# A graph network on one core: without the instructions that carry a second wait in the hot loops, and with the second tables' empty rows written in layer 1's first pass

## What is computed

```python
x = x + L0(h)   # gaussian mixture: msg = sum_k gauss_k(edge) * (h @ g)[src], mean over dst, + h @ root + bias
x = x + L1(h)   # two SAGE convolutions: mean of h[src] by dst, dense layers, relu, again
x = x + L2(h)   # spline convolutions: a small network moves each edge's coordinates,
                # then z[col*K + idx] weighted by an 8-corner basis, summed by row
x = x + L3(h)   # two SAGE convolutions with sums in place of means
```

## Time and profile before

| what | value |
|---|---|
| median of three timed runs | 15050.08 us (15047.9 to 15058.99) |
| the profiled execution's own time | 15074.62 us |
| its span, first to last instruction | 15072.8 us |
| mean granted TensorE clock | 0.558 of full speed |
| instructions in the profile | 155974 |
| busy: PE, DVE, ACT, POOL | 7096.2, 5575.7, 1755.8, 8971.3 us |

### The profile page before, as it was taken

How to read it: one execution, slowest core, us unless ns; L and a number is a source line. 1 busy time by engine, 2 the same in 40 slices (tenths; PEclk the granted TensorE clock), 3 DMA queues, 4 the chain that set the end, 5 groups by cost and what they waited for, 6 DMA issues and landing times. The chain is left out here.

```text
span 15072.8 us, 155974 instructions
## 1 busy us (share of the span) xinstructions
PE 7096.2 (47%) x32816; PEld 6021.4 (40%) x32819; DVE 5575.7 (37%) x11340; ACT 1755.8 (12%) x5296; POOL 8971.3 (60%) x9011
## 2 busy tenths in 40 slices
PE   5200455556665555455557775444444453334333
PEld 1100344446663333344446664433333343333332
DVE  8200344444445666333335554333233341111111
ACT  0000333322221111000010001111111110000000
POOL 0677566636665555555526665666666526664666
PEclk9555666655557777555555555555555555555555
DMA  7991111123331111211121112000111121112112
GB/s 271 139 106 13 53 67 67 64 70 91 89 86 34 42 41 40 26 30 31 30 13 12 12 12 15 12 12 12 21 23 23 24 34 12 12 12 12 13 13 14
DMA packets 790129, 641.91 MB, mean 43 GB/s; under 512 B 363646, under 2 KB 680304, under 8 KB 789814
## 3 DMA queue, kind: packets, MB, share of 16 engines
q1 hardware_dynamic: 466548, 303.70, 11.4%
q0 software_dynamic: 295168, 243.14, 9.1%
q10 hardware_dynamic: 28288, 93.72, 1.6%
HBM read 264.86 MB, written 386.20 MB: 43 GB/s over the span
## 5 line engine op out<-in xcount | busy, mean ns | idle before, releaser
L802 PE MATMUL ps<-got,oh 128*128 128x33 f32 x7040 | 1670.1, 400 | 2383.0 <-DVE oh L625 675.8
L802 PEld LDWEIGHTS ps<-got,oh 128*128 128x128 f32 x7040 | 1573.8, 327 | 2547.0 <-issue 2531.9
L765 POOL DMA_INDIRECT got<-q_table,idx x1760 | 1809.7, 1028 | 1186.1 <-DVE idx L807 657.2
L2144 POOL DMA_INDIRECT msg<-msg,idx x1792 | 1759.0, 982 | 1126.1 <-issue 524.4
L765 POOL DMA_INDIRECT got<-h_table,idx x1760 | 1719.1, 977 | 1116.8 <-issue 569.9
L1703 POOL DMA_INDIRECT cell<-rec,idx x880 | 921.6, 1047 | 609.4 <-ACT rec L1685 352.1
L348 POOL DMA_INDIRECT rec_r<-sc_rec,sc_idx x832 | 840.8, 1011 | 721.3 <-ACT sc_rec L339 423.2
L1367 POOL DMA_INDIRECT rec_d<-rec,idx x880 | 908.6, 1032 | 563.6 <-ACT rec L1307 310.5
L1969 POOL DMA_INDIRECT cell<-rec,idx x880 | 912.9, 1037 | 498.7 <-issue 270.8
L625 DVE TENSOR_TENSOR oh<-iota_f,rd 128x512 f32<-128x512 f32 x1105 | 759.7, 692 | 1025.1 <-DMA b<-in_L_gnn_b 498.2
L807 DVE CAST idx<-rd 128x4 int32 (+1 forms) x892 | 158.1, 178 | 2441.6 <-DMA msg<-msg,idx 634.8
(11 more groups left out here) (329 smaller groups left out, 13359.1 us busy)
## 6 DMA issues: line engine op xcount, KB each, us to landing
got<-rec_d SPq DMA_DIRECT2D x220, 416.0 KB
rec_d<-padd ACTq DMA_DIRECT2D x4, 11648.0 KB
rec_d<-padd ACTq DMA_DIRECT2D x4, 11232.0 KB
cin<-cell SPq DMA_DIRECT2D x224, 136.0 KB
msg<-msg,idx POOLq DMA_INDIRECT x1792
msg<-zpad SPq DMA_DIRECT2D x8, 3575.0 KB
got<-msg SPq DMA_DIRECT2D x220, 130.0 KB
cell<-rec,idx POOLq DMA_INDIRECT x1760
```

Of the source, the lines that this page charges most:

```text
L765: nc.gpsimd.indirect_dma_start(out=s["got"][:, n, g, :], out_offset=None, in_=table, in_offset=bass.IndirectOffsetOnAxis(ap=s["idx"][:, n, ...
L802: mm = nc.tensor.matmul(psum_rows[:, ds(at[g], W)], s["oh"][:, n, g, :], s["got"][:, n, g, 0:W], start=False, stop=False)
L2144: nc.gpsimd.indirect_dma_start(out=msgs, out_offset=bass.IndirectOffsetOnAxis(ap=idx[:, n, g:g + 1], axis=0), in_=msg[:, n, g, :], in_offs ...
```

## The change

Two things. First, every `sem_inc(tick, 1)` of PE, ACT and DVE in the loops named above goes; the waits stay. POOL's ticks stay, and those in `layer_norm` and the dense stages. Second, the scatter's phase now blanks only `cell1` and `msg1`; `cell2` and `msg2` are blanked by ACT with the same 16 DMAs, each waited for, at the start of its part of layer 1's first pass. The small source tiles `pad2` and `zpad` live through the whole kernel for that.

```diff
+        def blank_tables(eng, sem, tables):
+
+            parts, filled = 8, 0
+            for table, pad, tiles in tables:
+                groups = tiles // 2
+                view = table.rearrange("(p t u) w -> p t (u w)", p=P, u=2)
+                for q in range(parts):
+                    t0, t1 = groups * q // parts, groups * (q + 1) // parts
+                    eng.dma_start(view[:, t0:t1, :], bcast(pad.unsqueeze(1), [P, t1 - t0, pad.shape[1]])).then_inc(sem, 16)
+                    filled += 16
+                    eng.wait_ge(sem, filled)
...
-                    parts, filled = 8, 0
-                    for table, pad, tiles in ((cell1, ...), (msg1, ...), (cell2, ...), (msg2, ...)):
...
+                    blank_tables(sp, s_filled, ((cell1, pad1[:, :, :].rearrange("p u w -> p (u w)"), TC),
+                                                (msg1, zpad[:, 0:2 * (F1 + 1)], TILES_N)))
...
             def act(eng):
+                if blank is not None:
+                    blank_tables(eng, s_blank, blank)
                 if t_nm is None:
                     return
                 with eng.Fori(0, NI) as i:
...
                         eng.wait_ge(picked, k + R - 1)
-                        nc.scalar.sem_inc(tick, 1)
...
                 pe.wait_ge(s["gathered"][n], 16 * G * (i + 1))
                 pe.wait_ge(s["hot"], k + 1)
-                nc.tensor.sem_inc(tick, 1)
...
                 ins.then_inc(sem, 1)
                 v.wait_ge(sem, ops * i + at[0])
-                nc.vector.sem_inc(tick, 1)
             return then
...
-                    run_sums(job_sum_in_rows(e, h_table, C + 1, acc_nm), job_sum_out(e, msg1, F1, acc_s[:, :]))
+                    run_sums(job_sum_in_rows(e, h_table, C + 1, acc_nm, blank=((cell2, ..., TC), (msg2, ..., TILES_N))),
+                             job_sum_out(e, msg1, F1, acc_s[:, :]))
```

More of the change, by code:

```diff
@@ L733, in rows_keep, with job_sum_in_rows @@
                                       ps[:, q, 0:nb * AW].rearrange("p (b w) -> p b w", w=AW)).then_inc(s["kept"], 1)
-        def job_sum_in_rows(c, table, width, acc, t_nm=None, new=None):
+        def job_sum_in_rows(c, table, width, acc, t_nm=None, new=None, blank=None):
             W = AW
@@ L746, in job_sum_in_rows @@
                     "turned", "copied", "picked", "part", "new", "ranked", "rank_start"))
+            s_blank = sem_in(c, "blanked") if blank is not None else None
             def act(eng):
+                if blank is not None:
+                    blank_tables(eng, s_blank, blank)
                 if t_nm is None:
@@ L2300, in build @@
                 with ExitStack() as e:
-                    run_sums(job_sum_in_rows(e, h_table, C + 1, acc_nm), job_sum_out(e, msg1, F1, acc_s[:, :]))
+                    run_sums(job_sum_in_rows(e, h_table, C + 1, acc_nm, blank=((cell2, pad2[:, :, :].rearrange("p u w -> p (u w)"), TC),
+                                                                             (msg2, zpad[:, 0:2 * (F2 + 1)], TILES_N))),
+                             job_sum_out(e, msg1, F1, acc_s[:, :]))
                 next_phase()
```

38 lines of the change are left out of this document (1 added, 37 removed).

## The result

The changed kernel took 15034.08 us (median of 16 runs, 15012.66 to 15047.52) against 15060.86 us of the kernel before beside it: a ratio of 0.9981, 95% interval 0.9974 to 0.9989. It is faster, by 27 us where 137 were forecast. Two later comparisons on other chips gave 1.0004 (0.9993 to 1.0014) and 0.9993 (0.9984 to 1.0002), no measurable difference. The profiled execution took 15028.06 us; its span is 15026.2 us, 46.6 less than before's.

The account below looks back on a forecast made before the run. POOL's indirect DMAs and its waits, about once a turn, for late engines were taken to bound the kernel. Terms -42 - 30 - 20 - 75 + 5 + 25 = -137 us from 15050 gave 14,915 us, range 14,720 to 15,110.

Parts of the forecast that it names:

- rank_turn: Layer 1's second pass: 14 DVE ticks x 55 turns x 0.11 = 85 us; half taken, 42 us gain.
- the four rivals: Ticks free where it counts (0.15); blanks hold gathers (0.12); ticks stand in slow stretches (0.10); slow stretches move (0.08).
- to_cells: row_turn's DVE chain in to_cells: 10 ticks x 55 x 0.11 = 60 us; half taken, 30 us gain.
- sum_out_rows: One tick each of PE and ACT per batch, 220 batches: 24 to 48 us; 20 us gain taken.
- The seven others: Source, destination, both messages, layer 1's first, layer 3's two passes: 419 waits at 0.18 us, 75 us gain.
- The scatter: Blanks of cell2 and msg2 leave its phase: between 14 us cost and 10.9 us gain, +5 taken.
- The other bound: The scatter's phase: the gain of one stall of 10.9 us.
- The blanks: 16 DMAs moved into layer 1's first pass: between 0 and 174 us of cost, +25 taken.
- Rival 2: Layer 1's first pass: blanks delay gathers' landings, costing 106 to 174 us; kernel 15,105 to 15,175; chance 0.12.
- Rival 1: Ticks free where it counts: POOL's waits come from slow stretches of fixed length; 15,060 us; chance 0.15.

Follow-up runs that it names:

- key_only: The kernel before less the three ticks of rank_turn between the operations on `key` and `mark`; 1.0016 of the kernel before.
- rank_only: The kernel before less only the 14 ticks of rank_turn's chain; 0.9958 of the kernel before.
- keep_rank: The changed kernel with the ticks of rank_turn's chain put back; 0.9976 of the kernel before.
- t_only: The kernel before with the change's ticks out, the blanks of cell2 and msg2 left in the scatter's phase; 0.9978 of the kernel before.
- b_only: The kernel before with the blanks moved and all the ticks left in; 1.0007 of the kernel before.
- best_old: The changed kernel with PE's ticks back in the four passes of gathered rows and the blanks left in the scatter's phase; 0.9991 of the kernel before.
- rep_after2: The changed kernel again, unaltered, on another chip; 0.9993 of the kernel before.
- act_only: The kernel before less ACT's ticks alone (some 3800); 0.9986 of the kernel before.
- rep_before: One execution of the kernel before, unaltered, on a chip where POOL's waits are not there; 13134.66 us.

## Why the prediction was wrong

The direction was right, and the measured time lies within the range; the size was a fifth of what was said.

**The step that failed is rank_turn's: "the chain sits in DVE's queue in front of them", 42 us of gain.** Layer 1's second pass lost 47 us, and these 89 us are nearly all of the 90 between the forecast's 137 and the 46.6 of the two profiled executions. (Against the medians' 27 us, 110 were missing.) The size of a tick on DVE (0.11 us) was right. But the shorter chain shortened no wait: POOL's waits in that pass did not move (178.5 to 181.6). What moved was `mark` against POOL's restart, and the gathers took 43 us longer. That is in POOL's busy time, where none of the four rivals looked. key_only shows the hold with three ticks, and rank_only shows the same cause with the other sign, on a chip where POOL does not wait and the pass follows its busy time.

How much of the 47 us is rank_turn's own is not shown. The pass also lost ticks of PE and ACT. With those gone, taking rank_turn's out as well made the pass 12 us shorter (keep_rank 1411.6, t_only 1400.0), with 56 us more of POOL's time and 73 us less waiting. With those in place, three of rank_turn's ticks cost 24 us (key_only against b_only). PE's ticks alone, put back, changed nothing (best_old 1431.4, rep_after2 1430.3), and ACT's alone, taken out, little (act_only 1373.0). So the loss belongs to the ticks together, and with pauses POOL's holds and its waits trade against each other in a way that no run explains.

The reading that failed under it is the first one: POOL's mean time per DMA. I took 0.94 us for a calm gather from the timeline and did not ask why the page's groups say 977 and 1028 ns. Layer 1's second pass had 122 us of POOL's time over the median already, and that was the row to follow.

- *to_cells*: 30 forecast, 16.1 measured; right in sign. Its waits did not shrink; POOL was busy 21 us less.
- *sum_out_rows*: 20 forecast, 13.0 measured with what lies around it. By the profile only ACT's tick took an instruction with it there.
- *The seven others with layer 1's first pass's blanks*: -75 + 25 = -50 forecast, -55.6 measured (12.4, 9.8, 7.5, 11.8, 15.3, -3.7, 2.5). The sum held, and in part by luck: POOL's waits fell by 112 us and not by 75, its DMAs took 43 us longer, for which there was no term, and the 25 us for the blanks were not there (b_only).
- *The scatter*: +5 forecast, +1.1 measured with pauses; without, 10 us of gain, all of it in POOL's waits (42 to 32 us, busy 816 us in both). The other bound, a stall fewer, was the right one there.
- *The blanks*: +25 forecast. With pauses nothing shows; without, 33.9 us of waits, all beside msg2's blanks, and about 20 us net. Rival 2 named the mechanism, late landings, and put it at 106 to 174 us; the waits are a third of the lower figure. The landings were late by 8 us in the median and by 12 at most, and the ring's 20 us hid most of that (the hiding is argued, not shown). The page "DMA: Bandwidth & Descriptors" of the Trainium skill, with its turns between queues ("Queues, rings and completion order"), put this toward the low end, and the trace agrees: no batch took over 13.5 us to land while one blank DMA of msg2 takes some 25.
- *Rival 1* (ticks free where they count) has layer 3's lengths right, 1276.3 and 1273.6 us after, 1272.6 and 1276.1 before, but not their cause: the waits did fall, by 18 and 9 us, and POOL's DMAs took 19 and 4 us longer.

**The pauses.** I took a wait's 0.7 us per PE instruction for the cause. After the change PE has next to no such slow stretches in layer 3 (11 of its sequencer's instructions take 0.6 to 1.5 us in the first pass, 146 before, and none in the kernel before on a chip without pauses) and the waits stay. This is one pause in keep_rank's layer 1, second pass, by the timeline:

```profile
8303.55 1.09 PE L785 MATMUL ps<-ident,oh 128*128 128x128 f32 x4
...
8307.65 1.23 DVE L2173 TENSOR_TENSOR mark<-iota_f,key 128x1024 f32<-128x1024 f32 x1
...
8314.26 0.17 DVE L833 TENSOR_TENSOR part<-rd,ps 128x12 f32<-128x12 f32 x1 [5.39 <-remote]
8314.28 0.59 ACT L761 COPY oht<-ps 128x512 f32<-128x512 f32 x1 [13.14 <-DMA rec_d<-rec,idx]
...
8315.01 1.86 PE L795 MATMUL ps<-t_nm,oht 128*128 x8 [8.81 <-ACT oht L761]
```

PE's transposes end at 8304.64 by their modelled end; ACT, which waits for them, goes on at 8314.28, 9.6 us later and in the same instant as DVE, which waits for an earlier matmul. PE waits for ACT. DVE worked until 8308.88 and then stood for 5.39 us; two of its waiting instructions before that took 0.70 us, where the others took 0.02. POOL goes on starting gathers until it runs out of indices. The ends of PE's matmuls are modelled, so this does not tell whether PE itself was late or the engines that wait for it. Two of the five chips of the groups don't do this at all, and the kernel before takes 13,120 us there. What a pause is stays open. So does why layer 1's second pass was 1412 us in keep_rank, with its holds back at before's number.

## What to carry to other kernels

Where GpSimd's DMAs are the pace, look at their mean against their median before anything else: a shift of 0.1 us on another engine can put a vector operation with two SBUF inputs ahead of a DMA's start instead of behind it. Here that was worth 0.4 to 1 us each time, and up to 2 us behind the longest operation, in either direction. Taking an instruction out is then no pure saving; it is a new phase (another place in time against the other engines), to be measured stage by stage. Taking one of the two inputs from PSUM removed the hold; it saved no time on the chip where it was tried, where POOL's other waits took it up. And put a background transfer where the engine that paces does not need landings soon.

## What the runs showed of the hardware

- An indirect DMA of GpSimd took 0.946 us alone, 1.32 us behind a 0.69 us one-hot that started 0.19 us before it, and 1.97 us behind a 1.23 us comparison that started 0.07 us before it; a one-hot that started 0.03 us after it left it at 0.94. Behind a scan of 2.42 us with two inputs in SBUF it took 2.99 in the median and 3.13 at most (rep_before). A reduction of 1.97 us with one input held none: the 55 gathers that started during it took 0.944 in the median, 0.953 at most. With one of the one-hot's inputs in PSUM the mean of all 880 was 0.946. The Trainium skill ("SBUF — State Buffer", section "Who interferes with whom") says that a vector instruction with two SBUF inputs contends with GpSimd's reads, and that the order of issue decides; both agree with these rows, in which only the gather was ever held: a one-hot that started behind a gather kept its 0.69 us. It infers that `tensor_tensor` leaves the making of a DMA's descriptors alone; here an indirect DMA, which reads its indices from SBUF, is held by one.
- The kernel before took between 13,118 and 15,061 us (medians) on six chips. The same pair of kernels gave 0.9981 (0.9974 to 0.9989) on one and 1.0004 (0.9993 to 1.0014) on another, a gap as large as the effect.
- A batch's four gathers had landed 1.45 us (median) after the end of POOL's last instruction for them, and 9.3 us after it (13.5 at most) while DMAs of 1.8 MB, one at a time, ran on another queue.
